# A decoder block on one core: context keys stacked in two passes, input projection in fp32r parts, and a new order of the units between the attention heads

## The reference

```python
h  = x @ in_w.T + in_b                      # 256 -> 512 (input projection)
h  = silu(causal_conv4(h) + conv_b)
xp = h @ xp_w.T + xp_b
a  = exp(-exp(xp[..., :16]));  b = silu(xp[..., 16:]) * h.sum(-1)
state_t = state_{t-1} * a_t + b_t           # scan over the 256 tokens
x = layernorm(x + states @ out_w.T + out_b)
# attention: keys are 77 normalised context rows and the 256 latents themselves
ln = layernorm(x) * gl + bl;  kv = concat([layernorm(ctx) * gm + bm, ln])
out = softmax((ln @ Wq + bq) * 128**-0.5 @ k.T) @ v   # 8 heads of 128, 333 keys
x = layernorm(x + out @ Wo + bo)
# experts: 8, top 2 of 8, capacity 512 tokens for each; scatter-add of the results
x = layernorm(x + experts(x))
```

## Time and profile before

| | us |
|---|---|
| median of 3 runs (1080.32 to 1083.17) | 1081.81 |
| profiled execution, its own time | 1085.67 |
| its span, first to last instruction | 1083.5 |
| TensorE busy | 1020.0 (94%) |
| VectorE busy | 797.2 (74%) |
| ScalarE busy | 664.6 (61%) |
| GpSimd busy | 520.3 (48%) |

### The profile page before, as it was taken

One profiled execution on the slowest core, in us unless ns is written; L12 is line 12 of the kernel. 1 busy time (PEld: TensorE's weight loads), 2 busy tenths in 40 slices (PEclk: granted clock), 3 DMA queues, 4 the chain that ended last, 5 costly groups with the idle time before them and its releaser, 6 DMA issues.

```text
span 1083.5 us, 21193 instructions
## 1 busy us (share of the span) xinstructions
PE 1020.0 (94%) x7043; PEld 951.4 (88%) x7043; DVE 797.2 (74%) x2017; ACT 664.6 (61%) x1714; POOL 520.3 (48%) x830
## 2 busy tenths in 40 slices
PE   7899999999999999999999999999999999899970
PEld 5789999989899999999999999999999898889860
DVE  6787777877787778777877878777877766454526
ACT  5676666666666666666766576667665655155525
POOL 5623363735364535454545364635463543425653
PEclk8999999999999999999999999999999999999995
DMA  7562020112011211021111211031103000485448
GB/s 234 178 195 87 18 100 19 62 34 95 24 57 33 91 34 47 32 71 64 43 37 56 79 42 37 23 112 40 40 16 108 22 33 11 170 250 99 68 49 310
DMA packets 60366, 84.47 MB, mean 78 GB/s; under 512 B 13940, under 2 KB 43688, under 8 KB 60264
## 3 DMA queue, kind: packets, MB, share of 16 engines
q1 hardware_dynamic: 52584, 70.46, 19.5%
q0 software_dynamic: 7680, 12.72, 5.6%
HBM read 44.16 MB, written 38.99 MB: 77 GB/s over the span
## 4 chain that ended last, share of the span: by engine, by line
PE 75%; DVE 9%; ACT 9%; issue 3%; DMA 1%; POOL 1%; SPq 0%; ACTq 0%; DVEq 0%; POOLq 0%
PE ps L565 21%; PE ps L563 20%; PE ps L564 19%; PE ps L590 6%; PE ps L651 3%; PE ps L657 3%; DVE nmx L1453 2%; ACT prob L1028 1%; ACT fx L1100 1%; PE ps L695 1%; DVE cv L1166 1%; ACT k_hi L872 1%; DVE q_lo L1122 1%; PE ps L681 1%; ACT x2T L926 1%
## 5 line engine op out<-in xcount | busy, mean ns | idle before, releaser
L1661 POOL TENSOR_SCALAR prob<-prob,rinv 128x333 f32<-128x333 f32 x256 | 140.7, 561 | 352.5 <-DVE rinv L1462 351.8
L1023 ACT ACTIVATE oT_hi<-ps 128x256 fp32r<-128x256 f32 x128 | 49.2, 384 | 188.2 <-PE ps L565 188.2
L563 PE MATMUL ps<-kv_lo,w_hi 128*128 128x256 f32 (+1 forms) x512 | 159.1, 311 | 3.4 <-ACT x2T L926 1.0
L565 PE MATMUL ps<-kv_hi,w_hi 128*128 128x256 f32 (+1 forms) x512 | 153.5, 300 | 0.0
L564 PE MATMUL ps<-kv_hi,w_lo 128*128 128x256 f32 (+1 forms) x512 | 153.3, 299 | 0.0
L1028 ACT ACTIVATE prob<-ps,nmx 128x333 f32<-128x333 f32 x256 | 134.8, 536 | 13.2 <-DVE nmx L1453 13.1
L1108 DVE TENSOR_TENSOR pT_lo<-ps,pT_hi 128x512 fp32r<-128x512 f32 (+1 forms) x256 | 130.3, 551 | 0.6 <-ACT pT_hi L1040 0.6
L1453 DVE TENSOR_REDUCE nmx<-ps 128x2 f32<-128x666 f32 x128 | 108.6, 848 | 24.1 <-PE ps L565 23.1
L590 PE MATMUL ps<-ident,prob 128*128 128x128 f32 (+1 forms) x768 | 110.4, 273 | 6.5 <-DVE oT_lo L1108 5.7
L563 PE MATMUL ps<-pT_lo,v_hi 128*128 128x256 f32 (+1 forms) x384 | 108.5, 283 | 0.9 <-DVE pT_lo L1108 0.9
L565 PE MATMUL ps<-pT_hi,v_hi 128*128 128x256 f32 (+1 forms) x384 | 108.3, 282 | 0.0
(11 more groups left out here) (232 smaller groups left out, 3034.4 us busy)
## 6 DMA issues: line engine op xcount, KB each, us to landing
wraw<-in_W SPq DMA_DIRECT2D x14, 512.0 KB, 7.4
vcd_hi<-vst_hi SPq DMA_DIRECT2D x10, 512.0 KB, 2.7
vcd_lo<-vst_lo SPq DMA_DIRECT2D x10, 512.0 KB, 3.6
v_hi<-vcd_hi SPq DMA_DIRECT2D x32, 154.0 KB
v_lo<-vcd_lo SPq DMA_DIRECT2D x32, 154.0 KB
slots<-initr SPq DMA_DIRECT2D x8, 520.0 KB, 7.1
xs<-in_x SPq DMA_DIRECT2D x16, 256.0 KB
xts<-in_xT SPq DMA_DIRECT2D x15, 256.0 KB
```

Source lines behind the costliest of these rows:

```text
L563: pe.matmul(dst, hi1, lo2, start=first, stop=False, skip_group_check=True)
L565: return pe.matmul(dst, hi1, hi2, start=False, stop=last, skip_group_check=True)
L1023: act.activation(oT_hi[:, h % 2, :], ps[:, AVB, 0:S], ACT.Copy).then_inc(oTh_set, 1)
L1661: pool.tensor_scalar(prob[:, h % 2, t, 0:KEYS], prob[:, h % 2, t, 0:KEYS], rinv[:, h % 2, t:t + 1], 1.0, ALU.mult, ALU.mult).then_inc(norm ...
```

## The change

There are five parts.

1. **Context keys.** The third key block has 77 keys. Its three matmuls become two. In the first, 122 rows are contracted: the 77 high parts of the probabilities against the high values, and below them 45 copies of the high parts (keys 32 to 76) against the low values. In the second, 128 rows: 77 low parts against the high values, and in rows 96 to 127 the high parts of keys 0 to 31 against their low values. For that GpSimd copies 45 columns of `prob` to its end after each normalisation (`twice_set`), the transposes give 122 rows, ScalarE writes one more small part (32 partitions by 256) for each head, and the values of a batch come in four loads for each half instead of two.
2. **Input projection.** From the fourth sequence on (13 of 16) it uses `three` on parts: the weights are split once in the first batch, the rows of each batch by ScalarE (128x512) and GpSimd (128x512) in slot 2.
3. **Order.** Units, banks and side steps are placed anew: `v3` goes from slot 1 to slot 2, `x2T` from the front of slot 4 to its end, `cum` behind `q` and `v` in slot 7; at place N only a tap of the convolution (slot 0), the scan (slot 4) and `latents` (slot 5) are left; a new place E stands behind the slot's last units. The second half of the gate (`gt`, `inp`) is a side step of slot 3. GpSimd's `context_lo` goes from slot 3 to slot 2.
4. **Prologue.** VectorE takes one weight split from GpSimd, and does `mixed` (which feeds the first layernorm) ahead of the first value split; ScalarE does `ut` and `th2` ahead of `e1`.
5. **Sequencer work.** The increments of `need_apart` are gone, the expert loops of TensorE and GpSimd are unrolled, and the first expert's weights are loaded in batch 14 instead of batch 0.

```diff
-    [("k", 2, "att", 1), ("v", 2, "att", 0), ("v", 3, "att", 2)],
+    [("k", 2, "att", 1), ("v", 2, "att", 2)],
...
-                for j in range(KT):
-                    r, c = KROWS[j], slice(h * DH, (h + 1) * DH)
-                    last = three(ps[:, AVB, 0:S], v_hi[0:r, j, c], v_lo[0:r, j, c], pT_hi[0:r, j, :], pT_lo[0:r, j, :],
-                                 j == 0, j == KT - 1)
-                last.then_inc(av_mm, 1)
+                c = slice(h * DH, (h + 1) * DH)
+                for j in range(NT):
+                    three(ps[:, AVB, 0:S], v_hi[:, j, c], v_lo[:, j, c], pT_hi[:, j, :], pT_lo[:, j, :], j == 0, False)
+                r = KROWS[2]
+                pe.matmul(ps[:, AVB, 0:S], v_hi[0:r, 2, c], pT_hi[0:r, 2, :], start=False, stop=False,
+                          skip_group_check=True)
+                pe.matmul(ps[:, AVB, 0:S], v_lo[:, 2, c], pT_lo[:, 2, :], start=False, stop=True,
+                          skip_group_check=True).then_inc(av_mm, 1)
...
+                if name == "in" and bb > 2:
...
+                        for k in range(KD):
+                            last = three(g[:, c * S:(c + 1) * S], inw_hi[:, k, o], inw_lo[:, k, o],
+                                         xt_hi[:, k, :], xt_lo[:, k, :], k == 0, k == KD - 1)
...
-                        act.activation(pT_hi[0:CTX, 2, :], ps[0:CTX, T0 + 1, 0:S], ACT.Copy).then_inc(pTh_set, 1)
+                        act.activation(pT_hi[0:CTX + REST, 2, :], ps[0:CTX + REST, T0 + 1, 0:S], ACT.Copy)
+                        act.activation(pT_lo[96:P, 2, :], ps[0:32, T0 + 1, 0:S], ACT.Copy).then_inc(pTh_set, 1)
...
+                        need(pool, norm_set, 2 * n + 2)
+                        pool.tensor_copy(prob[:, h % 2, :, KEYS:PCOL], prob[:, h % 2, :, S + 32:KEYS]).then_inc(twice_set, 1)
...
+                    if h == 2 and "aft" in have and b:
+                        pool.wait_ge(xTh_set, b)
+                        pool.tensor_tensor(xt_lo[:], xts[:], ap(xt_hi[:]), ALU.subtract).then_inc(xTl_set, 1)
...
-                    if h == 3 and "ctx" in have:
+                    if h == 2 and "ctx" in have:
                         context_lo(tile)
...
-                split_lo([2, 3])
+                split_lo([3])
```

More of the change, by code:

```diff
@@ L42 @@
 KT = 3
-KROWS = [P, P, CTX]
+REST = CTX - 32
+KROWS = [P, P, CTX + REST]
+PCOL = KEYS + REST
 CT = -(-B * CTX // P)
@@ L69 @@
 OP = [u[0] for u in FLAT].index("op")
+XP = [u[0] for u in FLAT].index("xp")
 def need(eng, sem, value):
@@ L442, in values @@
                 c = slice(half * 512, half * 512 + 512)
-                for d, part in zip(vc_rows, (v_hi, v_lo)):
-                    sp.dma_start(ap(part[0:CTX, 2, c]), d[bass.ds(a, 1)].rearrange("o t n -> (o t) n")[:, c]
-                                 ).then_inc(vc_ld[half], 16)
+                hi, lo = [d[bass.ds(a, 1)].rearrange("o t n -> (o t) n") for d in vc_rows]
+                sp.dma_start(ap(v_hi[0:CTX, 2, c]), hi[:, c]).then_inc(vc_ld[half], 16)
+                sp.dma_start(ap(v_hi[CTX:CTX + REST, 2, c]), lo[32:CTX, c]).then_inc(vc_ld[half], 16)
+                sp.dma_start(ap(v_lo[0:CTX, 2, c]), hi[:, c]).then_inc(vc_ld[half], 16)
+                sp.dma_start(ap(v_lo[96:P, 2, c]), lo[0:32, c]).then_inc(vc_ld[half], 16)
             def first():
@@ L850, in _ @@
             outer(0, 0)
-            with pe.Fori(1, E // 2) as i:
-                inner(2 * i - 1, 1)
-                rows(2 * i, 0, 16 * i)
-                outer(2 * i - 1, 1)
-                inner(2 * i, 0)
-                rows(2 * i + 1, 1, 16 * i + 16)
-                outer(2 * i, 0)
+            for e in range(1, E - 1):
+                u = e % 2
+                inner(e, u)
+                rows(e + 1, 1 - u, 16 * ((e + 1) // 2 + (1 - u)))
+                outer(e, u)
             inner(E - 1, 1)
@@ L1216, in chosen, with gated @@
                                   ALU.is_equal).then_inc(mask_set, 1)
+            def gated(b, par, tile, g=bank(XP)):
+                a = b + 1
+                need(dve, th2_set, a + 1)
+                dve.scalar_tensor_tensor(out=gt[:], in0=th2[:], scalar=1.0, in1=ut[:], op0=ALU.add,
+                                         op1=ALU.mult).then_inc(gt_set, 1)
+                need(dve, gt_set, a + 1)
+                need(dve, e1_set, a + 1)
+                dve.scalar_tensor_tensor(out=inp[:], in0=gt[:], scalar=0.25, in1=g[64:64 + NST, 0:S],
+                                         op0=ALU.mult, op1=ALU.mult).then_inc(inp_set, 1)
             def state_lo(b, par, *tile):
@@ L1435, in _ @@
                 (2, "N"): [t_(3, 3)],
-            })
+                (2, "A"): [("nxt", lambda b, par, tile: silu(b + 1, 0))],
+                (2, "C"): [("prv", residual)],
+                (3, "N"): [("nxt", lambda b, par, tile: silu(b + 1, 1))],
+                (3, "A"): [("prv", residual_stats)],
+                (3, "C"): [("ctx", lambda b, par, tile: context_hi(tile))],
+                (3, "D"): [("nxt", gated)],
+                (4, "N"): [("nxt", scan)],
+                (4, "B"): [("nxt", state_lo)],
+                (4, "C"): [("nxt", mixed)],
+                (5, "N"): [("nxt", latents)],
+                (5, "A"): [u_(1, 1)],
+                (5, "B"): [u_(0, 1)],
+                (5, "C"): [u_(0, 2)],
+                (5, "E"): [u_(1, 2), ("prv", chosen)],
+                (6, "A"): [("prv", last_counts), ("nxt", latents_hi), ("prv", first_weight), ("prv", last_places)],
+                (7, "C"): [u_(0, 3)],
+                (7, "D"): [("prv", last_slots)],
+                (7, "E"): [u_(1, 3)],
+            }
             first()
@@ L1750, in _ @@
             add(0, 0)
-            with pool.Fori(1, E // 2) as i:
-                add(2 * i - 1, 1)
-                add(2 * i, 0)
-            add(E - 1, 1)
+            for e in range(1, E):
+                add(e, e % 2)
             for c in range(LC):
```

205 lines of the change are left out of this document (122 added, 83 removed), and 6 rows, old and new, of the table UNITS.

## The result

| | median us | ratio to before | 95% interval |
|---|---|---|---|
| before | 1081.32 (4 runs) | | |
| changed | 1074.26 (4 runs, 1073.6 to 1075.12) | 0.9942 | 0.9928 to 0.9955 |

The change is a gain of 7 us, not of 37. The profiled execution has a span of 1073.4 us. Later, on another chip, the changed kernel took 1074.32 us and the kernel before 1085.51 (ratio 0.9894, 0.9879 to 0.9909): the kernel before differs between chips by 0.4%, the changed one hardly. The trace of the kernel before is of an execution 4.3 us above its median (1085.67 us), that of the changed kernel of one 0.9 us above (1075.12), so a difference of these two traces is some 3.5 us too large.

The account below looks back on a forecast made before the run. TensorE was taken to bound the kernel, almost without gaps. Savings of 15.4 (context keys), 10.4 (input projection), 10.0 (order, net) and 1.2 (prologue) sum to 37.0 us, giving 1044.8 us; range 1034 to 1061.

Parts of the forecast that it names:

- the two tests that it set itself: Wrong if transposes in slots 1, 3 or 4 wait over 0.5 us, or batches 1 to 13 shrink under 1.8 us each.
- order and prologue, without new delays: Waits of TensorE that the new order removes, 16.4 us, and an earlier first batch through VectorE's freed scan, 1.2 us.
- context keys: One matmul fewer in each of 128 heads, 0.12 us each: 15.4 us, all on the path.
- input projection: 26 units in parts at 1.44 us instead of 1.84 in fp32: 10.4 us saved, lower bound 7.8.
- new delays: Late starts of slot 3 and delays of `nmx` and `oT_lo` in slot 4: 6.4 us lost.
- I put this at 0.4 us a batch, 6.4 us in 16: The size set for delays from VectorE's fuller slot 2 and slot 4's scan, with GpSimd's chain into slot 1 counted inside.
- GpSimd holds VectorE: Rival: GpSimd's row split stops VectorE work in slots 2 and 3, 1.2 us in 13 batches, 15.6 us; 1060.4; chance 0.07.
- the slack was worked out as short by 0.3 us: In slot 1, GpSimd's later `rank` chain and added copy exceed the 2.08 us ahead of head 0's transposes by 0.3 us.
- the order's 7.0 us: Slot 4's wait of `op` for `k_lo`, 7.0 us in 15 waits, goes with `k5` in bank 2.
- What is late next is the state itself: In slot 4, once `op` no longer waits for `k_lo`: state about 4.1 us after the slot's start, `in` ending at 4.8.
- What is taken from TensorE comes off the end: In batches 1 to 13 TensorE is busy 719.5 of 724.8 us; work added to other engines is hidden on average.
- The lower end of the range: 1034 us for the whole kernel, described as all bounds good.

Follow-up runs that it names:

- both_moves: The changed kernel with the second SiLU half of slot 2 right behind the first and `cum` between `q` and `v` in slot 7: 1051.67 us, ratio 0.973.
- changed_again: The changed kernel itself, run once more beside other kernels on another chip: 1074.32 us, ratio 0.9894 (kernel before 1085.51).
- d_cum_before_v: The changed kernel with the routing count `cum` between `q` and `v` of slot 7 instead of behind `v`: 1066.67 us, ratio 0.9835.
- c_scan_back: The changed kernel with the scan of slot 4 back at its place of before, behind `oT_lo`: 1074.07 us, ratio 0.991.
- before_two_passes: The kernel before with the two-pass context keys alone, its order unchanged: 1083.44 us, ratio 1.0023.

## Why the prediction was wrong

Right were the direction, what bounds the kernel, the end of the wait of `op` for `k_lo`, and the size of the prologue (1.9 us for 1.2, inside its bounds; the scan was freed, but `gt` is held in its place). The costs of ScalarE's second part (372 ns in the mean, 0.39 put down) and of GpSimd's copy (266 ns, 0.26 put down) were right, and in the new order both loads were hidden. Of the two tests that it set itself both failed: transposes wait over 0.5 us in slots 1 and 3, and the batches shrink by 0.65 us, not 1.8. The medians split the forecast of 37:

| term | predicted | measured |
|---|---|---|
| order and prologue, without new delays | 17.6 | 16.8 (1085.51 - 1068.71) |
| context keys | 15.4 | 11.8 (13.9 from the trace) |
| input projection | 10.4 | 4.2 |
| new delays | -6.4 | -22.3 (1074.32 - 1052.01) |

(The two middle terms are from the chip of both_moves, the others from that of changed_again.) The sum on the right is 10.5, and 1085.51 - 1074.32 = 11.2.

1. **The step that failed is the line "I put this at 0.4 us a batch, 6.4 us in 16".** It was a guess over three places; against both_moves they cost 0.88 us (slot 3), 0.54 us (slot 1) and 0.25 us (slot 4) in the mean of 13 batches, and the two moves that removed them gave 22.3 us.
2. **Slot 3 is the rival "GpSimd holds VectorE"**, with a chance of 0.07. Its mechanism, its operation and nearly its price (15.6 us for 13 batches; 11.2 measured with the split left out, 14.4 with the SiLU moved) came true. It was put aside with "most of VectorE's work in those places reads PSUM". That is so, but the argument needed the one operation that would stand beside `xt_lo`: `xt_lo` waits for `xt_hi`, ScalarE does this at the end of slot 2's queue, and there VectorE has the SiLU, with both inputs in SBUF. The rule of the Trainium skill, SBUF — State Buffer, "Who interferes with whom" (an operation of VectorE with two SBUF inputs contends with one of GpSimd that reads SBUF, and this is an exclusive lock), agrees with 1.62 against 0.68 us, and with `q_lo` unharmed; the prologue's scan had shown it in this very kernel. The same lock, `cx_lo` on `gt`, is most of slot 4's 0.25 us (0.36 us in each batch with a context tile). The prediction priced the VectorE load of slot 2 in busy time alone.
3. **Slot 1: the slack was worked out as short by 0.3 us** and hidden in the 0.4. The place and the sign were right; the loss was 0.54. Missing was that three of the small operations, moved beside VectorE's taps, take 0.40 to 0.49 us instead of 0.20 (0.57 us in all against d_cum_before_v), and that three margins under 1 us were treated as one small sum. Those in slots 1 and 3 are paid in full in every batch.
4. **The input projection counted 0.30 us twice.** The 1.84 us from `in` to `op` hold a wait of `op` for `k_lo`, which the order's 7.0 us also claimed. In slot 6 no `op` follows. TensorE of the kernel before there, then of both_moves:

```profile
531.33 1.89 PE L651 MATMUL ps<-xts,inw 128*128 128x256 f32 x8
532.87 0.47 PE L563 MATMUL ps<-w_lo,oT_hi 128*128 128x256 f32 x1
```

```profile
510.73 0.36 PE L574 MATMUL ps<-xt_lo,inw_hi 128*128 128x256 f32 x1
...
512.23 0.28 PE L574 MATMUL ps<-w_lo,oT_hi 128*128 128x256 f32 x1
```

   The unit takes 1.54 us there in fp32 and 1.50 in parts; with the next matmul, which is slower to follow an fp32 one (0.30 us to its successor in the kernel before, 0.12 in parts), and a start 0.08 us sooner behind the transposes, slot 6 differs by 0.28 us. In slot 4 what is saved ahead of `op` is mostly spent by `q` waiting for `k_lo`. Even the lower bound, 7.8, was too high.
5. **Slot 4.** "What is late next is the state itself" was wrong. The state is there 4.5 us into the slot, and `op` starts at 5.4 without waiting for it. What is late next is `k_lo` once more, now ahead of `q`, which follows `k5` in bank 2. That the scan at N makes `oT_lo` late was right, but this wait costs nothing of its own, as c_scan_back shows: `q` would wait for `k_lo` instead.
6. **"What is taken from TensorE comes off the end"** holds only if no other queue is full at a place where TensorE needs it. before_two_passes shows the other case: 0.12 us less in each head, and no gain, because ScalarE's added part, priced against 19.4 us of idle time in a batch, stands ahead of what `q` and `q_lo` wait for.
7. **The lower end of the range**, 1034, is no sum of the bounds that the prediction states: these (6.4, 1.0 and 0.7 us better) give 1036.7. Nothing hangs on it.

The forecast of 1044.8 is 7 us below both_moves (1051.7 and 1052.0): a kernel with these parts, and without the two waits.

## What to carry to other kernels

Before adding a GpSimd pass over SBUF, find which VectorE operation will stand beside it: one with both inputs in SBUF waited for the rest of the pass in these runs, and all in its queue with it. Where TensorE is dense and each slot is released by another queue, write for each moved step the slack of the next release, slot by slot, and count every one below 1 us at its full size per batch; a lump for "some delays" hides exactly the term that decides. When a wait is gone, ask which unit takes that bank next: the wait may only have moved. And take a unit's length where nothing waits behind it.
